# Expert stage of a four-part transformer block: every expert for every token, or tokens sorted by expert first

## What is computed

```python
logits  = x @ Wg                        # 2048 tokens x 8 experts
probs   = softmax(logits)
combine = one_hot(argmax(probs)) * probs
y       = einsum('bsh,ehd->bsed', x, W) + b        # every expert, W is 8 x 256 x 256
out     = einsum('bsed,bse->bsd', y, combine)      # all but one expert weighted by 0
result  = layernorm(x + out)
```

## Time and profile before

| | |
|---|---|
| median of 3 runs | 1126.92 us (1121.12 to 1128.57) |
| the profiled execution: its time, its span | 1126.6 us, 1124.9 us |
| TensorE busy | 983.8 us, 87% |
| VectorE, ScalarE, GpSimd busy | 657.6, 442.2, 248.9 us |
| L2081, matmuls of the experts | 116.1 us busy, 256 records |
| L2161, weighting on VectorE | 61.9 us busy, 128 instructions |
| mean granted TensorE clock | 0.849 |

### The profile page before, as it was taken

One profiled execution on the slowest core, in us unless ns is written; L12 is line 12 of the kernel. 1 busy time (PEld: TensorE's weight loads), 2 busy tenths in 40 slices (PEclk: granted clock), 3 DMA queues, 4 the chain that ended last, 5 costly groups with the idle time before them and its releaser, 6 DMA issues. The chain is left out here.

```text
span 1124.9 us, 21485 instructions
## 1 busy us (share of the span) xinstructions
PE 983.8 (87%) x8083; PEld 615.6 (55%) x8083; DVE 657.6 (58%) x2085; ACT 442.2 (39%) x997; POOL 248.9 (22%) x496
## 2 busy tenths in 40 slices
PE   6866726899699999989998999698999997999997
PEld 3545715777555555559863555344555554844442
DVE  1874793555477777544335255305777773747665
ACT  2553501000026666632228755532666663620000
POOL 1761112455413333310012000000333335000000
PEclk9985558555569999997889989696999999989998
DMA  5145533422200720020000000000000002000000
GB/s 115 33 80 121 189 105 100 93 59 68 49 1 16 194 57 1 1 86 1 1 21 5 1 1 1 1 0 1 2 2 2 1 1 76 1 1 19 20 15 23
DMA packets 48543, 43.96 MB, mean 39 GB/s; under 512 B 8668, under 2 KB 41784, under 8 KB 48184
## 3 DMA queue, kind: packets, MB, share of 16 engines
q1 hardware_dynamic: 41832, 36.81, 12.5%
q10 hardware_dynamic: 6128, 4.21, 1.6%
q0 software_dynamic: 480, 1.57, 0.5%
HBM read 23.57 MB, written 14.81 MB: 34 GB/s over the span
## 5 line engine op out<-in xcount | busy, mean ns | idle before, releaser
L814 DVE CUSTOM_DVE_ANT_0 l_masked_scores<-psum,mask_q_rows 128x384 bf16<-128x384 f32 (+3 forms) x512 | 225.0, 488 | 76.6 <-PE psum L761 75.8
L836 ACT ACTIVATE l_probs<-psum 128x512 f32<-128x512 f32 (+1 forms) x384 | 186.3, 526 | 150.2 <-PE psum L747 149.5
L849 POOL TENSOR_SCALAR_AFFINE_SELECT l_probs<-l_probs 128x256 f32<-128x256 f32 x256 | 101.4, 408 | 379.9 <-ACT l_probs L836 379.8
L761 PE MATMUL psum<-kb_heads,q_heads 32*128 32x384 f32 (+3 forms) x512 | 108.9, 508 | 10.7 <-DVE l_neg_max_rows L803 8.7
L2081 PE MATMUL psum<-expert_w,rows_32k 128*128 128x512 f32 x256 | 116.1, 607 | 1.2 <-PEq L44 1.2
L761 PE MATMUL psum<-l_k_heads,l_q_heads 32*128 32x384 f32 (+3 forms) x512 | 109.3, 509 | 4.6 <-DVE l_neg_max_rows L803 2.7
L747 PE MATMUL psum<-l_q_and_max,l_k_heads 32*128 32x256 f32 (+3 forms) x512 | 112.3, 472 | 0.0
L747 PE MATMUL psum<-l_q_and_max,kb_heads 32*128 32x256 f32 (+3 forms) x512 | 111.9, 470 | 0.0
L779 PE MATMUL psum<-l_probs,rows_32k 128*32 128x512 f32 (+3 forms) x1024 | 97.3, 458 | 2.9 <-POOL l_probs L849 2.9
L747 PEld LDWEIGHTS psum<-l_q_and_max,l_k_heads 32*128 32x128 f32 x512 | 58.8, 188 | 52.1 <-ACT l_probs L836 42.4
L747 PEld LDWEIGHTS psum<-l_q_and_max,kb_heads 32*128 32x128 f32 x512 | 58.5, 187 | 51.6 <-ACT l_probs L836 41.7
(11 more groups left out here) (316 smaller groups left out, 1650.5 us busy)
## 6 DMA issues: line engine op xcount, KB each, us to landing
gram_scratch<-rows_32k SPq DMA_DIRECT2D x4, 1024.0 KB, 4.8
rows_32k<-v_new_and_ones SPq DMA_DIRECT2D x64, 64.0 KB, 2.6
x_rows<-in_L_attn_x_dram SPq DMA_DIRECT2D x16, 128.0 KB, 7.1
heads_scratch<-rows_32k SPq DMA_DIRECT2D x2, 1024.0 KB, 5.4
heads_scratch<-q_kb_T SPq DMA_DIRECT2D x2, 1024.0 KB, 5.7
inverse_scratch<-block_inv SPq DMA_DIRECT2D x2, 1024.0 KB, 4.0
q_heads<-heads_scratch SPq DMA_DIRECT2D x2, 1024.0 KB, 7.0
ent_w<-in_L_ffn_ent_w_dram SPq DMA_DIRECT2D x2, 1024.0 KB
```

The source lines that it names most:

```text
L761: mm = nc.tensor.matmul(ps[:, row_bank(G, u, i), o:o + w], QT(b, gq)[r, t * P:(t + 1) * P], KT(b, gq)[r, 0:w], start=True, stop=True)
L814: last = nc.vector.tensor_tensor_reduce(out=junk[:, ROW_AT[G, u] % 2, i, o:o + w], in0=ps[:, row_bank(G, u, i), o:o + w], in1=g.maskq[:, N ...
L836: nc.scalar.activation(PT[:, G % 2, 2 * (u % 2) + i, o:o + w], ps[:, e_bank(G, u, i), 0:w], ACT.Exp, scale=SCALE).then_inc(x_ok, 1)
L849: last = nc.gpsimd.affine_select(out=d, in_=d, pattern=[[0, 2], [1, P]], compare_op=ALU.is_ge, fill=0.0, base=0, channel_multiplier=-1)
```

## The change

Each tile of 128 rows goes through one expert only. For that the tokens are sorted by expert into a scratch tensor in HBM, `sorted_d`, with room for NTS = 16 + 7 = 23 tiles (each expert's tokens begin on a tile of their own, so up to 23 tiles are needed).

- The projection stage writes its normalized rows into `XR`, 16 x 258 numbers to a partition: the row, and room for the gate's weight and the row number. GpSimd also clears a tile of zeros after the fourth bias addition, and SP stores it six times to clear `sorted_d` (3 MB in all). SP loads a table of constants, `route`, and the biases now go to one partition.
- The expert stage first finds a slot for each token: TensorE counts, for each token and expert, the tokens before it (16 matmuls that accumulate, 128 down to 8 columns) and then all tokens of each expert (one matmul); VectorE takes nine steps like those of before and then eight more to the slots, and four to the expert of each of the 23 tiles.
- GpSimd then issues 16 indirect DMAs, one for each tile, that write the 258 numbers of each of 128 rows to its slot. When all have landed, SP and ACT load the 23 sorted tiles with 11 DMAs (one tile each at first, then two, then three or four).
- For each of the 23 tiles: two transposes, ScalarE copies them, TensorE loads the tile's expert number into a register, makes two matmuls of 256 columns with the weights at that place and one with the bias of one partition; VectorE makes the row number an integer, weights and adds to the residual in one instruction, and makes the layer norm's statistics; ScalarE takes the root and normalizes; GpSimd issues an indirect DMA that writes the 128 rows to their places of the output. Slots that no token has carry a row number out of bounds and are not written.

Its core:

```diff
 phase_out_proj:
+            sp.wait_ge(zero_ok, 1)
+            for i in range(NZERO):
+                sp.dma_start(bass.AP(tensor=g.sorted_d.tensor, offset=g.sorted_d.offset + i * P * ZW, ap=[[ZW, P], [1, ZW]]), zero[:, :]).then_inc(g.zero_st, 16)
...
+            sp.wait_ge(g.zero_st, 16 * NZERO)
...
-                    ln.apply_act(act, c - 5, g.X[:, c - 5, :], g.X[:, c - 5, :])
+                    ln.apply_act(act, c - 5, g.XR[:, c - 5, 0:D], g.X[:, c - 5, :])
...
+                if c == 3:
+                    nc.gpsimd.memset(zero[:, :], 0.0).then_inc(zero_ok, 1)
 phase_moe:
+NTS = NT + E - 1
+XW = D + 2
+LOADS = [(t, 1) for t in range(4)] + [(t, 2) for t in range(4, 12, 2)] + [(12, 4), (16, 4), (20, 3)]
...
         def _(pe):
-            def experts(c):
...
-                    for k in range(KD):
-                        last = nc.tensor.matmul(ps[:, YB[n % len(YB)], :], xT[:, c, k, :], We[:, k, 2 * e2:2 * e2 + 2, :].rearrange("p e n -> p (e n)"),
-                                                start=(k == 0), stop=(k == KD - 1))
...
+            pe.wait_ge(gt, 6)
+            pe.wait_ge(or_ok, E + 1)
+            nc.tensor.matmul(ps[:, 0, 0:NT * E], before, oh[:, :, :].rearrange("p c e -> p (c e)"), start=True, stop=False)
+            for c in range(NT - 1):
+                last = nc.tensor.matmul(ps[:, 0, (c + 1) * E:NT * E], ones[:, :], bcast(oh[:, c, :], [[0, NT - 1 - c], [1, E]]), start=False, stop=(c == NT - 2))
+            last.then_inc(pre_ps, 1)
+            pe.wait_ge(gt, 7)
+            nc.tensor.matmul(ps[:, 1, 0:E], ones[:, :], cs[:, :], start=True, stop=True).then_inc(cnt_ps, 1)
+            pe.wait_ge(expert_ok, 1)
...
+            def sortedT(t):
+                pe.wait_ge(x_ld[load_of[t]], 16)
...
+                if t >= 2:
+                    pe.wait_ge(t_sb, t - 1)
+                for k in range(KD):
+                    last = nc.tensor.transpose(ps[:, 2 + t % 2, k * P:(k + 1) * P], xs[:, t, k * P:(k + 1) * P], g.idf[:, :])
+                last.then_inc(t_ps, 1)
+
+            def product(t):
+                e = pe.value_load(expert[0:1, t:t + 1], min_val=0, max_val=E - 1)
+                pe.wait_ge(t_sb, t + 1)
+                if t >= 2:
+                    pe.wait_ge(u_ok, t - 1)
+                for k in range(KD):
+                    nc.tensor.matmul(ps[:, 4 + t % 2, 0:D], xT[:, t % 2, k, :], We[:, k, bass.ds(e, 1), :].rearrange("p e n -> p (e n)"), start=(k == 0), stop=False)
+                nc.tensor.matmul(ps[:, 4 + t % 2, 0:D], ones[0:1, :], be[0:1, bass.ds(e, 1), :].rearrange("p e n -> p (e n)"), start=False, stop=True).then_inc(y_ps, 1)
+
+            sortedT(0)
+            for t in range(NTS):
+                if t + 1 < NTS:
+                    sortedT(t + 1)
+                product(t)
...
         def _(act):
+            act.wait_ge(sorted_st, 16 * NT)
+            for i, (t0, n) in enumerate(LOADS):
+                if i % 2:
+                    act.dma_start(xs[:, t0:t0 + n, :], g.sorted_d[t0 * P:(t0 + n) * P].rearrange("(t p) n -> p t n", p=P)).then_inc(x_ld[i], 16)
+            for t in range(NTS + 3):
+                if t < NTS:
+                    act.wait_ge(t_ps, t + 1)
+                    if t >= 2:
+                        act.wait_ge(y_ps, t - 1)
+                    nc.scalar.copy(xT[:, t % 2, :, :], ps[:, 2 + t % 2, 0:KD * P].rearrange("p (k m) -> p k m", k=KD)).then_inc(t_sb, 1)
+                if 1 <= t <= NTS:
+                    ln.std(act, t - 1)
+                if 3 <= t:
+                    s = t - 3
+                    if s >= 4:
+                        act.wait_ge(out_st[s % 4], 16 * (s // 4))
+                    ln.apply_act(act, s, yo[:, s % 4, :], xs[:, s, 0:D])
...
         def _(pool):
+            pool.wait_ge(slot_ok, 1)
+            for c in range(NT):
+                nc.gpsimd.indirect_dma_start(out=g.sorted_d, out_offset=bass.IndirectOffsetOnAxis(ap=slot[:, c:c + 1], axis=0), in_=XR[:, c, :], in_offset=None,
+                                             bounds_check=NTS * P - 1, oob_is_err=False).then_inc(sorted_st, 16)
+            for t in range(NTS):
+                pool.wait_ge(ln.y_ok, t + 1)
+                pool.wait_ge(row_ok, t + 1)
+                nc.gpsimd.indirect_dma_start(out=g.out.rearrange("b n d -> (b n) d"), out_offset=bass.IndirectOffsetOnAxis(ap=row[:, t:t + 1], axis=0), in_=yo[:, t % 4, :], in_offset=None,
+                                             bounds_check=B * N - 1, oob_is_err=False).then_inc(out_st[t % 4], 16)
...
         def _(dve):
...
+            for t in range(NTS + 2):
+                if t < NTS:
+                    dve.wait_ge(x_ld[load_of[t]], 16)
+                    nc.vector.tensor_scalar(row[:, t:t + 1], xs[:, t, D + 1:D + 2], -1.0, float(2 * B * N), ALU.mult, ALU.add).then_inc(row_ok, 1)
+                    dve.wait_ge(y_ps, t + 1)
+                    nc.vector.scalar_tensor_tensor(out=xs[:, t, 0:D], in0=ps[:, 4 + t % 2, 0:D], scalar=xs[:, t, D:D + 1], in1=xs[:, t, 0:D], op0=ALU.mult, op1=ALU.add).then_inc(u_ok, 1)
+                if 1 <= t <= NTS:
+                    ln.rstd(dve, t - 1)
+                if t < NTS:
+                    dve.wait_ge(u_ok, t + 1)
+                    ln.stats(dve, t, xs[:, t, 0:D])
+                if 1 <= t <= NTS:
+                    ln.shift(dve, t - 1)
+                if t < NTS:
+                    ln.mean_var(dve, t)
```

More of the change, by code:

```diff
@@ L2055, in phase_moe @@
-        st = g.out_stored
+        We, be, XR, rt = g.We, g.be, g.XR, g.route
+        lim, below, tile_no, row_no, before = (rt[:, ROUTE[i]:ROUTE[i + 1]] for i in range(5))
+        lg, pr, oh = sb("logits", [P, NT, E]), sb("exps", [P, NT, E]), sb("choice", [P, NT, E])
+        mxl, sm, first = sb("max", [P, NT]), sb("sum", [P, NT]), sb("first_rank", [P, NT])
+        cs, cm, tl, tm, st, en = (sb("tile_choices", [P, E]), sb("over_limit", [P, E, NT]), sb("tiles", [P, E]), sb("tiles_below", [P, E, E]), sb("first_tile", [P, E]), sb("end_tile", [P, E]))
@@ new lines, in phase_moe @@
+        pf, pos, slot = sb("slots", [P, NT, E]), sb("slot", [P, NT]), sb("slot_int", [P, NT], I32)
+        te, expert = sb("tiles_past", [P, NTS, E]), sb("tile_expert", [P, NTS], I32)
+        ef = sb("tile_expert_f", [P, NTS])
+        order, ones = sb("order", [P, E]), sb("ones", [P, P])
+        xs, row = sb("sorted_rows", [P, NTS, XW]), sb("row_int", [P, NTS], I32)
+        xT, yo = sb("sorted_T", [P, 2, KD, P]), sb("out_rows", [P, 4, D])
+        or_ok, gt, ex_ok, id_ok, pre_ps, cnt_ps, slot_ok, expert_ok = (sem("order_ok"), sem("gate_steps"), sem("exps_ok"), sem("row_numbers"), sem("before_psum"), sem("count_psum"),
+                                                                      sem("slots_ok"), sem("experts_ok"))
@@ L2062, in _ @@
         @block.sync
         def _(sp):
[L2064 to L2068, removed]
+            sp.wait_ge(sorted_st, 16 * NT)
+            for i, (t0, n) in enumerate(LOADS):
+                if i % 2 == 0:
+                    sp.dma_start(xs[:, t0:t0 + n, :], g.sorted_d[t0 * P:(t0 + n) * P].rearrange("(t p) n -> p t n", p=P)).then_inc(x_ld[i], 16)
@@ L2070, in _ @@
+            for i in range(4):
+                sp.wait_ge(out_st[i], 16 * ((NTS + 3 - i) // 4))
         @block.tensor
         def _(pe):
[L2072 to L2083 removed]
@@ L2085, in biases @@
[L2085 to L2089, removed]
-            pe.wait_ge(g.we_ld, 16 * (1 + E))
[L2092 to L2100, removed]
@@ L2141, in _ @@
-            dve.wait_ge(ex_ok, 1)
[L2142 to L2175, removed]
+            n = [0]
+            def step(ins):
+                n[0] += 1
+                ins.then_inc(gt, 1)
+                dve.wait_ge(gt, n[0])
+            dve.wait_ge(g.logits_ps, 1)
@@ L2269, in consts @@
                                  np.where((q // R == own // HD % B) & (q % R // CH == own // (B * HD)), 1, 0)], 1).astype(np.float32),
+        "route": np.concatenate([np.tile(P * np.arange(NT), (P, 1)), np.tile(np.tril(np.ones((E, E)), -1).reshape(1, -1), (P, 1)), np.tile(np.arange(NTS), (P, 1)),
+                                 2 * B * N - (N * (q // R) + R * np.arange(NT)[None, :] + q % R), q < k], 1).astype(np.float32),
         "ones": np.ones((1, N), np.float32),
```

94 lines of the change are left out of this document (53 added, 41 removed).

## The result

The changed kernel takes 1118.14 us (median of 20 runs, 1109.24 to 1125.6), the kernel before 1129.33 in its 20 (1121.12 to 1135.76): ratio 0.990, 95% interval 0.988 to 0.992. It is faster, by 1%, where 2.3% was forecast. The profiled execution has a span of 1114.7 us.

What follows compares the result with a forecast made beforehand. The prediction took TensorE to bound the old expert stage (136.0 us) and the VectorE-ScalarE circle the new loop. From 988.9 us, its terms summed to 1099.5 us span, + 1.7 giving 1101 us, 2.3% less; range 1075 to 1127.

Steps and rivals of the forecast that it cites:

- to the slots: Expert stage's beginning: gate steps, 17 float32 counting matmuls at 8.3 us, eight VectorE steps; 13.0 us from the stage's start.
- 23 tiles and the cold start: Expert loop: 23 tiles at 2.6 us, 59.8 us, plus 2.0 us for starting at a low clock.
- tail: Behind the last product: last layer norm 2.5 us, output scatter 4.1, 0.8 to the span's end; 7.4 us.
- The start is cold: Start of the 23-tile loop: TensorE begins at a low clock, costing + 2.0 us once.
- rival (b): TensorE's clock stays low throughout the loop: 3.3 us a tile, 14 us more, 1115 us; chance 0.09.
- The circle through VectorE and ScalarE: Loop: product, VectorE's weighting and statistics, ScalarE's root, normalizing and copy, next product; 4.4 us for two tiles, 2.2 each.
- (a): Queue work is cheaper and hides: indirect DMA 0.8 us, loop 2.15 us a tile; 19 us less, 1082; chance 0.17.
- (d): GpSimd's descriptor making bounds scatter and loop: meets 1126.6 us at 2.7 us per indirect DMA, slower above; chance 0.09.
- Rival (e): TensorE's register load and addresses stand in the open: 1.1 us more per loop tile, 25 us, 1126; chance 0.09.
- my 0.4 for the register and GpSimd's part together: Loop: allowance per tile for TensorE's register and addresses plus GpSimd's output DMA delaying VectorE's shift; 0.4 us.
- Rival (c): Each GpSimd output DMA holds up VectorE's shift in the loop: 3.2 us a tile, 14 more, 1115; chance 0.11.
- my + 0.9: Before the expert stage: GpSimd's clearing of zeros lengthens VectorE's stall at the shift; 0.9 us, between nothing and 1.

Runs made afterwards that it cites:

- experiment 1: Changed kernel with the experts' one-row bias matmul left out of the loop of 23 tiles: 1078.95 us, ratio 0.952 against the kernel before.
- experiment 3: Changed kernel with the loop's bias matmul over 128 rows (127 with zero weights) instead of one: 1085.68 us, ratio 0.966 against the kernel before.
- experiment 2: Changed kernel plus 24 discarded 512-column matmuls while tokens are sorted, so the loop begins at full clock: 1085.18 us, ratio 0.963 against the kernel before.
- experiment 5: Changed kernel plus only 8 discarded wide matmuls, followed by idle time before the loop: 1116.66 us, ratio 0.995 against the kernel before.
- experiment 7: Changed kernel plus 27 discarded wide matmuls, bias over 128 rows, bfloat16 counting with the total ahead: 1078.78 us, ratio 0.964 against the kernel before.
- experiment 4: Changed kernel with each tile's expert fixed at build time, no register load: 1121.89 us, ratio 0.994 against the kernel before.
- experiment 6: Changed kernel plus 24 discarded wide matmuls before the loop and each tile's expert fixed at build time: 1088.4 us, ratio 0.971 against the kernel before.

## Why the prediction was wrong

The sum of the prediction against the profiled execution, term by term (us of span):

| term | predicted | measured | difference |
|---|---|---|---|
| start of the stage | 989.8 | 985.8 | -4.0 |
| to the slots | 13.0 | 11.8 | -1.2 |
| GpSimd's start after the slots | 0 | 1.0 | +1.0 |
| 16 indirect DMAs | 20.8 | 20.3 | -0.5 |
| last landing | 2.8 | 1.5 | -1.3 |
| load of the first tile | 2.9 | 2.7 | -0.2 |
| first transposes and copy | 1.0 | 1.2 | +0.2 |
| 23 tiles and the cold start | 61.8 | 79.3 | +17.5 |
| tail | 7.4 | 11.1 | +3.7 |
| sum | 1099.5 | 1114.7 | +15.2 |

**The step that failed** is the sentence of the forecast "The start is cold: 16 records took 9.05 instead of 7.06 us at the stage's start, + 2.0", and behind it the case against rival (b): "at the low clock TensorE would be busy nearly all the time with wide matmuls, and after such a beginning it rose". TensorE was busy all the time, as said there; the clock did not rise. In the sum it is the + 2.0 that failed: with the measured pitches the low clock cost 23 x (3.46 - 2.06) = 32 us. What I took from the earlier trace rows was a start made of 512-column matmuls over 128 rows only. In the loop 1.15 of 3.47 us are a matmul over one row. Without it, or with 128 rows in its place, the clock rises (experiments 1 and 3); with it a loop that begins at 0.50 stays there, and one that begins at 1.00 stays at that (experiment 2). Rival (b) named what happened, its pitch of 3.3 us was 5% short (with the measured 3.46 it gives 1119 instead of 1115, and 1118.14 was measured; that this is so near is luck in part, since the stage began 4.0 us early and the tail took 3.7 more). I gave it 0.09 because I read "busy" in the rows as if all busy time were alike. The window in the earlier trace rows that I put forward for (b), with TensorE busy for less than half of 5 us, was not the case that came: there was no idle time in the loop.

The Trainium skill, TensorE: Matmul & The Clock Gate, section Part 1: The HAM clock gate (the "warmup" mystery), says that the throttled state is the default and that activity releases it. Experiment 5 agrees with the first half: the clock was back at 0.50 before the loop began, after wide matmuls and a wait. With the second half experiments 1 and 3 agree. The changed kernel does not, if the busy time of the records is taken for activity: 79.3 us of it released nothing.

**What held, and what the low clock hid.** With the clock at 1.00 the loop is faster than predicted, 2.06 us a tile against 2.6. The term of 61.8 us, at the full clock, would have been 23 x 2.06 = 47.4, so that its miss of 17.5 is two: 31.9 too little for the clock and 14.4 too much for the rest. With the clock at 1.00 the span would have been 1114.7 - 79.3 + 47.4 = 1083 us, 1085 of time, and experiment 2 measured 1085.18; the forecast of 1101 would have missed that too, by 16. The circle through VectorE and ScalarE, worked out at 2.2 us, is 1.97 where it is the bound (experiment 7). The indirect DMA, which I bounded between 0.5 and 3 us and took at 1.3, is 1.28: rivals (a) and (d) are out, though (a)'s pace of 2.15 is near the 2.06 of experiment 2. Rival (e) is out with 0.04 us a tile (experiments 4 and 6), and of my 0.4 for the register and GpSimd's part together little more is to be seen. The `tensor_load` floor of about 600 ns, which the Trainium skill gives in DMA: Bandwidth & Descriptors, section Latency and other measured facts, does not appear in the open here: experiments 2 and 6 differ by 0.04 us a tile. Rival (c) is out too: the shift takes 143 ns beside 23 indirect DMAs. The contention that the Trainium skill states in GPSIMD Engine Reference, section Key points, shows beside GpSimd's additions, and not beside its indirect DMAs.

**Smaller misses.** The clearing of the zeros takes 0.93 us on GpSimd, as forecast, but it did not lengthen the stall of that shift. In this execution it all but went (rows answering to the earlier trace rows):

```profile
951.92 0.28 DVE L891 SCALAR_TENSOR_TENSOR l1p_neg_mean_rstd<-l1p_mean_var,l1p_rstd 128x1 f32<-128x1 f32 x1
```

In the execution of experiment 3, with the same cleared tile, it was 3.70 us, and ended again just where GpSimd's run did. So 2.82 was one draw of something that varies, and neither my + 0.9 nor the 3.1 us by which the stage began earlier is an effect that these runs show to belong to the change. The counting took 7.4 us where I had 8.3: 34 weight loads at 0.22 us instead of 0.245.

The tail is longer, and this I had not worked out:

```profile
1102.38 1.22 PE L2123 MATMUL psum<-expert_b,moe_ones 1*128 x2
...
1108.97 0.97 POOL L2170 DMA_INDIRECT out_dram<-moe_out_rows,moe_row_int  x1 [0.30 <-issue]
```

The last three tiles are normalized one after another only when the last root is there, and each then waits for an indirect DMA of 1.28 us, so that GpSimd's last one begins 5.4 us after the last product ends instead of about 2.5; 0.8 us of the 5.4 lie between the end of the first of these three normalizings and the start of its DMA. From its end at 1109.94 to the end of the span are 4.8 us, where a landing is 2.4 us from the issue; what the rest is the trace does not show, and I did not try it.

## What to carry to other kernels

When a change puts a wait in front of a stretch of matmuls, ask in which clock the stretch begins and whether its own mix can lift it from there; "TensorE busy 100%" does not answer that, the granted clock does. If part of the mix uses few rows (a bias over one row, say), either spread it over all rows, which cost no more here (0.43 us against 0.62), or keep TensorE at work with discarded wide matmuls until just before the first real one (1.0 us before in experiment 2; a few too many hold it up, as in experiment 7): each of the two alone was worth some 30 us here, nearly three times what the whole change had brought. A cost that no row shows deserves its bounds, but the largest miss came from a row that was shown and read for a case it did not cover.

## What the runs showed of the hardware that I had not expected

- The same loop has two stable paces, 3.46 us a tile at clock 0.50 and 2.06 at 1.00, and it keeps the one in which it starts (20 runs of the changed kernel between 1109 and 1126 us, four of experiment 2 between 1076 and 1090; the pace itself is read from one execution of each).
- The clock went to 1.00 within 6 us of the loop's start when the bias matmul ran over 128 rows with 127 rows of zero weights (experiment 3), and not in the whole loop when it ran over one and the loop began at 0.50.
- A one-row float32 matmul with 256 columns takes longer in the loop than one over 128 rows: 0.62 us against 0.43 from its start to the next operation's at the full clock, 1.15 against 0.85 at half. In the former the queue of weight loads stands idle before its loads and before those of the next transposes, 0.33 us each at the full clock and 0.65 at half (experiments 2, 3 and 7, and the changed kernel). Why is not shown.
- An indirect DMA of 128 rows costs GpSimd 1.28 us (1032 bytes a row on the way in, 1024 on the way out), 2.5 times a direct one of the earlier trace rows, and the output DMAs land 2.0 to 2.7 us after their issue.
- A load of an expert number into a register of TensorE for each tile, with three addresses made from it, costs 0.04 us in the open at the full clock and none at half (experiments 2, 4 and 6).
- 17 counting matmuls took 7.4 us in float32 and 1.1 us in bfloat16, at the same clock of 0.50.
